# Routed FFN tile loop: the expert's down-projection columns fetched by SyncE's DMA with a register offset instead of copied by VectorE

## What is computed

```python
def _swiglu(x, wg, wu, wd):
    return jax.nn.silu(x @ wg.T) * (x @ wu.T) @ wd.T
shared_out = _swiglu(x, shared_gate, shared_up, shared_down)
logits = x @ gate_w.T
top_id = jnp.argmax(logits, axis=-1)
score = jax.nn.sigmoid(jnp.max(logits, axis=-1))
xs = x * score[:, None]
def body(acc, ws):
    wg, wu, wd, e = ws
    xe = jnp.where((top_id == e)[:, None], xs, 0.0)
    return (acc + _swiglu(xe, wg, wu, wd), None)
routed_out, _ = jax.lax.scan(body, acc0, (r_gate, r_up, r_down, jnp.arange(E)))
```

## Time and profile before

| | |
|---|---|
| median of three runs | 706.99 us (705.5 to 707.17) |
| the profiled execution | 707.51 us |
| its span, first to last instruction | 705.7 us |
| PE, DVE, ACT, POOL busy | 77%, 79%, 46%, 38% |
| mean granted TensorE clock | 0.892 of full speed |

### The profile page before, as it was taken

How to read it: one execution, slowest core, us unless ns; L and a number is a source line. 1 busy time by engine, 2 the same in 40 slices (tenths; PEclk the granted TensorE clock), 3 DMA queues, 4 the chain that set the end, 5 groups by cost and what they waited for, 6 DMA issues and landing times. The chain is left out here.

```text
span 705.7 us, 12640 instructions
## 1 busy us (share of the span) xinstructions
PE 545.4 (77%) x3880; PEld 403.7 (57%) x3880; DVE 557.9 (79%) x1825; ACT 326.1 (46%) x712; POOL 271.2 (38%) x243
## 2 busy tenths in 40 slices
PE   0689999999999999999776887950598313587991
PEld 0355677767777777777555467940355213445981
DVE  5979999999999999998997674577589998663552
ACT  0357667766776677667432215722243100112760
POOL 2044433443344334433302782650134542035562
PEclk9999999999999999999996688985699765589997
DMA  9908200000000000000003012239000000002224
GB/s 301 356 1 150 33 1 3 1 2 2 2 2 1 1 3 1 2 1 2 2 0 98 18 50 57 89 86 145 1 0 1 0 0 0 1 22 65 59 77 141
DMA packets 33490, 31.35 MB, mean 44 GB/s; under 512 B 4608, under 2 KB 30336, under 8 KB 32896
## 3 DMA queue, kind: packets, MB, share of 16 engines
q1 hardware_dynamic: 28464, 23.44, 13.5%
q0 software_dynamic: 2560, 5.26, 2.2%
q10 hardware_dynamic: 2400, 1.84, 0.8%
HBM read 20.80 MB, written 9.74 MB: 43 GB/s over the span
## 5 line engine op out<-in xcount | busy, mean ns | idle before, releaser
L432 POOL TENSOR_TENSOR att<-att,small 128x512 f32<-128x512 f32 x64 | 81.5, 1273 | 197.8 <-ACT att L345 197.7
L475 PE MATMUL banks<-qexp,qkT 64*128 64x512 f32 x256 | 74.2, 656 | 0.3 <-DVE att L664 0.3
L345 ACT ACTIVATE att<-banks 128x512 f32<-128x512 f32 x64 | 38.2, 597 | 64.5 <-PE banks L475 64.5
L948 POOL DMA_INDIRECT rows_back<-ffn_yt,ffn_xt x48 | 49.5, 1031 | 44.5 <-DVE ffn_yt L1209 43.3
L1073 PE MATMUL banks<-ffn_xtT,ffn_wt 128*128 128x128 f32 x384 | 55.4, 291 | 0.0
L381 ACT ACTIVATE qexp<-qkT,small 128x256 f32<-128x256 f32 x128 | 54.6, 497 | 1.1
L450 POOL TENSOR_TENSOR qk<-cosq,sinq 128x512 f32<-128x512 f32 x32 | 45.7, 1429 | 20.2 <-DVE sinq L709 20.2
L1073 PEld LDWEIGHTS banks<-ffn_xtT,ffn_wt 128*128 128x128 f32 x384 | 50.2, 204 | 1.0 <-issue 0.4
L941 POOL DMA_INDIRECT rows_in<-ffn_xs,ffn_slot x32 | 37.0, 1157 | 33.8 <-DVE ffn_slot L1167 24.7
L664 DVE TENSOR_TENSOR att<-banks,small 128x512 f32<-128x512 f32 x64 | 44.0, 687 | 5.7 <-PE banks L475 5.7
L1203 DVE TENSOR_TENSOR ffn_hr<-ffn_silr,banks 128x256 f32<-128x256 f32 x48 | 20.2, 421 | 29.6 <-ACT ffn_silr L988 14.8
(11 more groups left out here) (228 smaller groups left out, 1425.2 us busy)
## 6 DMA issues: line engine op xcount, KB each, us to landing
rows_in<-zero_rows SPq DMA_DIRECT2D x2, 1548.0 KB, 14.9
ffn_xt<-rows_in SPq DMA_DIRECT2D x48, 64.5 KB, 1.9
rot<-in_rot SPq DMA_DIRECT2D x3, 1024.0 KB, 12.0
routed_sb<-in_routed SPq DMA_DIRECT2D x1, 3072.0 KB, 11.6
rdec_tab<-power_rows SPq DMA_DIRECT2D x16, 128.0 KB, 7.3
ffn_yg<-rows_back SPq DMA_DIRECT2D x8, 256.0 KB, 7.6
rot<-in_rot ACTq DMA_DIRECT2D x1, 1024.0 KB, 12.0
w<-in_W SPq DMA_DIRECT2D x2, 512.0 KB, 7.3
```

The source lines that it names most:

```text
L345: act.activation(att[:, c, HALF:HEADS], b_att[:, HALF:HEADS], ACT.Copy) \
L432: pool.tensor_tensor(att[:, c, HALF:HEADS], att[:, c, HALF:HEADS], spread(causal.unsqueeze(1), 1, HALF), ALU.mult) \
L475: ins = pe.matmul(b_att[:, 4 * hh:4 * hh + 4, :], qkT[rows, v, 1, c], qexp[rows, v % 2, c], start=True, stop=True)
L948: pool.indirect_dma_start(rows_back, bass.IndirectOffsetOnAxis(ap=token, axis=0), yt[:, j % RING], None).then_inc(stored[j % RING], 16)
```

## The change

- The DVE stream of the FFN no longer copies the down columns. SP does it: for tile t it reads the expert's number into a register and issues a DMA from `routed_sb` to the ring buffer, SBUF to SBUF, 128 partitions by 1 KB.
- For the first six tiles (all of the ring) this stands ahead of SP's wait for the scatter, behind a wait for `expert_ready`. For tiles 6 to 23 it stands in step t ahead of the x load of the same tile, with the wait for `y_psum` of tile t-6.
- PE no longer waits for the DVE copy ahead of the gate and up matmuls. It waits for the DMA (`down_loaded`, one semaphore for each of six buffers) ahead of the down matmuls, three steps after the transposes.
- The kernel needs five more semaphores. `retention` hands back its 52, and in call 0 POOL clears each of them with an instruction of its own, behind `decays` and ahead of the wait for `slot_ready`. The clearing at the end of `oscillator` covers six more and one less.

```diff
             def _(sp):
                 if tables:
                     tables.load(sp)
+                sp.wait_ge(s["expert_ready"], 1)
+
+                def weights(t):
+                    e = sp.value_load(expert_of[0:1, t:t + 1], min_val=0, max_val=EXPERTS - 1)
+                    wait(sp, s["y_psum"], t - WT_RING + 1)
+                    sp.dma_start(wt[:, t % WT_RING, ACT_COLS:], w["routed"][:, bass.ds(e, 1), ACT_COLS:]) \
+                      .then_inc(down_loaded[t % WT_RING], 16)
+
+                for t in range(WT_RING):
+                    weights(t)
                 sp.wait_ge(s["scattered"], 16 * NCH * (call + 1))
 
                 def step(t, u, k, on):
+                    if WT_RING <= t < TILES:
+                        weights(t)
                     if on(0):
...
                 if tables:
                     tables.decays(pool)
+                for one in used_up:
+                    pool.sem_clear(one)
                 pool.wait_ge(s["slot_ready"], 1)
...
                         wait(pe, s["wt_ready"], j + 1)
-                        wait(pe, s["wt_rest"], j + 1)
                         wait(pe, s["xtT_ready"], j + 1)
...
                         wait(pe, s["hr_ready"], j + 1)
+                        wait(pe, down_loaded[j % WT_RING], j // WT_RING * 16 + 16)
                         for f in range(2):
...
-                def weights(t):
-                    e = dve.value_load(expert_of[0:1, t:t + 1], min_val=0, max_val=EXPERTS - 1)
-                    wait(dve, s["y_psum"], t - WT_RING + 1)
-                    dve.tensor_copy(wt[:, t % WT_RING, ACT_COLS:], w["routed"][:, bass.ds(e, 1), ACT_COLS:]) \
-                       .then_inc(s["wt_rest"], 1)
-
-                for t in range(AHEAD):
-                    weights(t)
-
                 def step(t, u, k, on):
...
-                    if t + AHEAD < TILES:
-                        weights(t + AHEAD)
                 run(step)(dve)
```

More of the change, by code:

```diff
@@ L132, in build @@
         loaded_ffn = sem("loaded_ffn")
-        retention(nc, a, xin, resid, stats, (eye, causal, block, headmask, decay), small, banks,
-                  loaded_x, loaded_small, ffn_w, rows_in, token_ids, loaded_ffn)
+        retention_sems = retention(
+            nc, a, xin, resid, stats, (eye, causal, block, headmask, decay), small, banks,
+            loaded_x, loaded_small, ffn_w, rows_in, token_ids, loaded_ffn)
         tabs = {"cos": sb("cos_tab", [P, 2, T]), "dec": sb("dec_tab", [P, 2, T]),
@@ L143, in build @@
             ffn(nc, 0, xin, stats, ffn_w, rows_in, rows_back, token_ids, eye, route, banks, loaded_ffn,
-                ffn_sems, tables, None)
+                ffn_sems, tables, None, retention_sems)
         oscillator(nc, a, xin, stats, eye, banks, ow, tabs, ffn_sems)
         ffn(nc, 1, xin, stats, ffn_w, rows_in, rows_back, token_ids, eye, route, banks, loaded_ffn,
-            ffn_sems, None, outs)
+            ffn_sems, None, outs, [])
 def rsqrt_steps(eng, v, y, tmp, chain, count, done, out):
@@ L820, in _ @@
                 run(step)(dve)
+    return list(s.values())
 def ffn_semaphores(nc, ctx):
@@ L828, in ffn_semaphores @@
              "gu_ready", "silr_ready", "hr_ready", "y_psum", "yt_ready",
-             "added", "out_stored", "wt_ready", "wt_rest")
+             "added", "out_stored", "wt_ready")
     one = {n: ctx.enter_context(nc.semaphore("ffn_" + n)) for n in names}
@@ L834, in ffn_semaphores @@
     ring["x_loaded"] = [ctx.enter_context(nc.semaphore(f"ffn_x_loaded{r}")) for r in range(XT_RING)]
+    ring["down_loaded"] = [ctx.enter_context(nc.semaphore(f"ffn_down_loaded{r}")) for r in range(WT_RING)]
     return {"one": one, **ring}
@@ L842, in clear_ffn_semaphores @@
             pool.sem_clear(one)
-    for one in sems["x_loaded"] + sems["gathered"]:
+    for one in sems["x_loaded"] + sems["down_loaded"] + sems["gathered"]:
         pool.sem_clear(one)
 def ffn(nc, call, x, stats, w, rows_in, rows_back, token_ids, eye, route, banks, loaded_ffn, sems, tables,
-        outs):
+        outs, used_up):
     BLK = 4
@@ L880, in ffn @@
         hs = sb("hs", [P, 2, 2, 512])
-        s, x_loaded, stored, gathered = (sems[n] for n in ("one", "x_loaded", "stored", "gathered"))
+        s, x_loaded, down_loaded, stored, gathered = (
+            sems[n] for n in ("one", "x_loaded", "down_loaded", "stored", "gathered"))
         xt = sb("xt", [P, XT_RING, ROW])
```

## The result

The changed kernel takes 721.88 us (median of 4 runs, 719.98 to 725.89) where the kernel before takes 706.4 (median of 4): 1.0227 times as long, interval 1.0178 to 1.0276. The prediction said 710.0 us, 706.5 to 716.5. It is slower, as forecast, but five times as much: +15.5 us, not +3.

The account below looks back on a forecast made before the run. The loops were taken as near PE's pace, stalled by late stores and x loads through eight x buffers. Clears 1.0 plus 2 x 1.0 for the loops gave +3.0 us: 710.0 us as median, range 706.5 to 716.5.

Parts of the forecast that it names:

- SP's step: SP's work per tile in the loops: register load, weight DMA and x load take 1.49 us, against PE's 1.45.
- 1.0 us a loop: Both tile loops: net loss from later x loads, 1.4 us less 0.4 for shorter stores.
- The upper bound: SP's step in the loops at the highest prices: 1.80 us a tile, +4.5 and +3.0 us for the two loops.
- rival C: Tile loops: SP becomes the bound at 1.80 us a tile, 7.5 us plus 1.0 for clears, 715.5 us; chance 0.14.
- the difference is stalls: Tiles 4 to 23 before the change: 1.8 and 3.3 us beyond PE's pace are stalls on late x loads behind stores.
- a ring with less slack: Eight x buffers in the loops: some 0.3 of 0.7 us slack goes, so late landings stall PE more; chance 0.50.
- Cost removed from the path: 0: DVE's 48 weight copies in the loops: nobody waits for them, so removing them saves 0.
- 0.4 us a loop: POOL's stores in the loops: each stored tile returns 0.1 us earlier, a gain of about 0.4 us a loop.
- The 52 clears at 1.0 us: POOL in call 0: clears behind the last power delay the scatters and the loop, 1.0 us from 0.7 to 1.3.
- its case for a cost of 0: POOL in call 0: the clears cost 0 if the sequencer clears while the powers still run.
- Hidden additions: Six early weight DMAs (6.1 us), weight landings, DMA load and five clears behind the oscillator: covered or inside the bounds.
- Signs foretold: SP busy through both loops at 1.45 to 1.5 us a tile, PE idle up about 1 us a loop, DVE some 14 us less busy.

Follow-up runs that it names:

- e7_dram: Changed kernel with the down weights read from their DRAM tensor instead of the SBUF copy, register load kept in each step: 713.07 us, 1.0074 of the kernel before.
- after_ring12: Changed kernel with 12 x buffers in place of 8: 729.72 us, 1.0123 of the kernel before.
- e2_no_late_copies: Kernel before with DVE's weight copies for the first six tiles only, later tiles using stale weights: 720.16 us, 0.9993 of the kernel before.
- e6_x_first_hoist: Changed kernel with the x load first in SP's step and 18 register loads per call moved out of the steps: 707.19 us, 1.001 of the kernel before.
- e4_hoist: Changed kernel with 18 register loads per call moved out of SP's steps, weight DMA still first: 729.08 us, 1.0112; repeated in another group 711.2 us, 1.0055.
- the larger ring with both edits: Changed kernel with x load first, register loads out of the steps and 12 x buffers in place of 8: 725.9 us, 1.0078 of the kernel before.
- e3_static: Changed kernel with a fixed expert in the weight DMA and no register load: 724.59 us, 1.0061 of the kernel before.

## Why the prediction was wrong

- **The step that failed is SP's step, "0.66 + 0.32 + 0.04 + 0.43 + 0.04 = 1.49 us".** It measures 1.90. The register work is 0.73 where 0.66 stood, so ACT's row was a fair guide. The weights' issue is 0.50 where 0.32 was taken, and the x load behind it 0.59 where 0.43 was: 0.18 and 0.16 of the missing 0.41. Both prices had come from DMAs that read DRAM; e7_dram shows that they hold for those, and that an SBUF source changes both. Of 1.90 the excess over PE is 0.45, of 1.49 it would have been 0.04.
  This, and not the clears, is the term that was mis-sized: "1.0 us a loop" measured 7.7 and 8.2.
- **The upper bound was none.** "Both issues at 0.43" gave 1.80 us a step. The highest price in sight was taken for the highest possible, though rival C itself said that no row shows SP issuing a DMA from SBUF.
- **What SP's excess costs was also put too low.** Rival C let the present stalls be covered by it. By that reckoning 19 steps of 0.45 less stalls of 1.8 and 3.3 give +12 us in the loops; measured between tiles 4 and 23 is +16.7. Nor were those 5.1 us all waits for a late x load, as "the difference is stalls" has it: PE's transposes behind tile 4 wait for one in 2.1 us of them, by the trace of the kernel before. In the changed kernel a late load isn't covered: SP is not ahead. Call 1 has two, of 3.6 and 4.0 us, and 40.0 us instead of 36.1.
- **The mechanism taken as likeliest, a ring with less slack, was wrong; C's was right.** SP waits in the loops for no store at all, and 12 slots change nothing (after_ring12). What it does wait for is tile 0's down matmuls, once a call, ahead of tile 6's weights (5.0 and 3.7 us), in call 0:

```profile
SPq L916 <- PE banks L1100: 5.0, 1, 5.0
```

  So it goes into its 1.90 us steps with six tiles loaded where eight were before.
- **"Cost removed from the path: 0" was right** (the trace of the kernel before, e2_no_late_copies and e6_x_first_hoist), and so was the shorter store, 0.97 us in place of up to 1.09; but its 0.4 us a loop weren't there, since SP no longer waits for a store. The rule of the Trainium skill, "SBUF — State Buffer", section "Who interferes with whom", on which the prediction drew here, agrees with these stores in kind; POOL is no bound here, so nothing hangs on it.
- **The 52 clears at 1.0 us came out near in size, by luck.** Against the 27.6 us without them, 0.9 to 1.5 in twelve traces, 2.3 in one, and 0.1 to 0.2 in three, the profiled one among them. But the prediction had them start behind the last power, end at 399.4 and push the first scatter to 399.7. They ran from 393.0 to 396.9, the first half of them beside the last powers, close to its case for a cost of 0, and the first scatter went out at 397.89; what is left comes from the 0.92 us between the last clear and the first scatter, which the prediction had at 0.3.
- **Hidden additions were right**: the six early weight DMAs end at 417.6, 7 us ahead of the first x load; the weights land in 2.0 us and PE never waits for them; the bytes cost nothing that e6_x_first_hoist shows.
- Signs foretold: SP busy through both loops, yes, but at 1.90; PE's idle grown, by far more; DVE 14.5 us less busy.

The Trainium skill, "DMA: Bandwidth & Descriptors", section "Latency and other measured facts", would have given an estimated 8 us by its floor of about 600 ns for a `tensor_load`. That is nearer to the result than my 3, but not for its reason: the load measures 0.33 us here.

Left open: what makes a group one of the 720 us kind; why e4_hoist costs 1.1% there and 0.55% in the other, and why the larger ring with both edits is slower there than the kernel before; and why an SBUF source makes the next issue longer too.

## What to carry to other kernels

Before handing a queue one more job per step, add up its whole step from issue prices of the same kind of DMA (source memory included), and compare it with the bound's step: here 1.90 us against 1.45 cost 2%, 1.58 cost 0.7%, and a step below 1.45 with the awaited load first 0.1%, which is no difference. Moving work off an engine with slack gained nothing, though it freed 14.5 us of it. If it must move, put the transfer that someone waits for first, hoist register loads to where the queue is idle, and read from DRAM where the data also lies there.

## What the runs showed that was not expected

- SP takes 0.32 us to issue an x load out of idleness, 0.43 behind one from DRAM, 0.59 behind one from SBUF; a 128-row DMA from DRAM 0.34, from SBUF 0.47 with a fixed and 0.50 with a register's offset, 0.49 also with 64 bytes a row. In `e3_static` the early ones from SBUF, each right behind another from SBUF, take 0.60.
- The late x loads of the changed kernel (issued at 441.85, 663.56, 678.02 and 694.08, landing in 2.7, 3.0, 3.6 and 4.0 us) each have a 16 KB instruction packet of 1.0 to 1.6 us beside them (441.65, 663.29, 679.56, 695.33), by the trace's packet records; so have two more that took over 2.5 us (457.96 and 695.98), and only one such load, at 444.28, has none. That this makes them late is suggested, not shown.
- The cost of one edit differs from group to group: with the register loads hoisted +7.4 and +8.5 us where the kernel before takes 720.6, +3.7 where it takes 707.5.
